# In layer 1, the reciprocals of the softmax sums and their store each move ahead of one step of x's quantisation

## The reference

```python
# layer 1, attention: 16 heads of 64, keys and values from ctx and one null key
attn = softmax(q * scale @ k.T)          # sums over 129 keys
out  = layernorm((attn @ v) @ Wo)
x = x + out
# layer 1, feed-forward: 128 -> 512 -> 128, rows quantised to 127 steps by their own largest value
def act_quant(x):
    s = 127 / clip(max(|x|, axis=-1), 1e-5)
    return clip(round(x * s), -128, 127) / s
x = x + bitlinear(silu(bitlinear(xn, w_gate)) * bitlinear(xn, w_up), w_down)
```

## Time and profile before

| what | value |
|---|---|
| median of 3 runs | 813.28 us (813.21 to 814.16) |
| the profiled execution, its own time | 821.97 us |
| its span | 820.2 us, mean granted TensorE clock 0.975 |
| TensorE (PE) busy | 775.9 us, 95% |
| VectorE (DVE) busy | 661.5 us, 81% |
| GpSimd (POOL) busy | 479.6 us, 58% |
| ScalarE (ACT) busy | 436.1 us, 53% |
| a_rT, the 32 reciprocals | 950 ns each, first at 338.5 us, last at 793.8 us |

### The profile page before, as it was taken

One profiled execution on the slowest core, in us unless ns is written; L12 is line 12 of the kernel. 1 busy time (PEld: TensorE's weight loads), 2 busy tenths in 40 slices (PEclk: granted clock), 3 DMA queues, 4 the chain that ended last, 5 costly groups with the idle time before them and its releaser, 6 DMA issues.

```text
span 820.2 us, 28896 instructions
## 1 busy us (share of the span) xinstructions
PE 775.9 (95%) x10878; PEld 655.3 (80%) x10908; DVE 661.5 (81%) x1747; ACT 436.1 (53%) x1049; POOL 479.6 (58%) x912
## 2 busy tenths in 40 slices
PE   8999999998898997999999999999999999999983
PEld 6777777776698996888888888888888888888861
DVE  6888989877756664578889888888898888988876
ACT  4666666656065773445455554554554545545542
POOL 7767678887856773335554654654655646555234
PEclk9999999989999999999999999999999999999995
DMA  8986220000421211112132231231221222213110
GB/s 245 374 331 255 102 86 15 16 21 28 142 72 49 64 50 36 38 50 64 48 77 57 54 81 47 54 82 46 67 69 48 81 52 55 81 48 76 42 39 14
DMA packets 72892, 66.76 MB, mean 81 GB/s; under 512 B 28354, under 2 KB 53682, under 8 KB 72754
## 3 DMA queue, kind: packets, MB, share of 16 engines
q1 hardware_dynamic: 57890, 40.66, 18.0%
q10 hardware_dynamic: 12816, 20.06, 6.6%
q0 software_dynamic: 2048, 4.20, 1.7%
HBM read 35.89 MB, written 24.37 MB: 73 GB/s over the span
## 4 chain that ended last, share of the span: by engine, by line
PE 49%; DVE 22%; SPq 11%; DMA 10%; issue 5%; ACT 1%; POOL 1%; DVEq 1%; another core or an unknown queue 0%; POOLq 0%; ACTq 0%
DMA a_r_all<-a_r_rows 7%; SPq L1483 4%; PE psum L1039 4%; PE psum L432 4%; PE psum L421 3%; DVE a_mxf L2231 3%; PE psum L1027 3%; PE psum L414 3%; PE psum L1807 3%; SPq L1462 3%; PE psum L1915 3%; PE psum L1881 2%; SPq L1467 2%; PE psum L1834 2%; DVE f_h L2317 2%
## 5 line engine op out<-in xcount | busy, mean ns | idle before, releaser
L2090 ACT ACTIVATE a_pT<-psum 128x512 f32<-128x512 f32 x128 | 69.5, 594 | 63.4 <-PE psum L1902 41.1
L1589 POOL TENSOR_TENSOR f_hd<-f_hmc,a_wmean 128x1 f32<-128x1 f32 x32 | 6.8, 212 | 135.5 <-DVE f_hr L2328 134.3
L720 DVE TENSOR_REDUCE l_mx<-psum 128x4 bf16<-128x512 f32 x128 | 81.8, 681 | 4.5 <-PE psum L403 2.9
L2231 DVE TENSOR_REDUCE a_mxf<-psum 128x8 f32<-128x1024 f32 x64 | 77.5, 1210 | 5.3 <-PE psum L1871 5.3
L1807 PEld LDWEIGHTS psum<-a_xT,a_Wq 128*128 128x128 f32 x512 | 66.5, 197 | 18.2 <-issue 14.1
L1819 PEld LDWEIGHTS psum<-a_cTm,a_Wk 128*128 128x128 f32 x512 | 64.3, 192 | 13.9 <-issue 13.9
L552 ACT ACTIVATE l_pT<-psum 128x512 f32<-128x512 f32 x128 | 70.6, 597 | 8.5 <-PE psum L421 8.2
L1807 PE MATMUL psum<-a_xT,a_Wq 128*128 128x128 f32 x512 | 73.2, 288 | 0.6 <-ACT a_xT L2073 0.6
L1583 POOL TENSOR_SCALAR f_hq<-f_ht 128x512 bf16<-128x512 f32 x31 | 60.4, 1947 | 19.9 <-ACT f_ht L2133 19.8
L1881 PE MATMUL psum<-a_qT,a_kT 64*128 64x128 f32 x1024 | 71.5, 280 | 0.0
L1849 PE MATMUL psum<-a_Wv,a_cTm 128*128 128x512 f32 x128 | 69.7, 630 | 0.0
(11 more groups left out here) (315 smaller groups left out, 2075.4 us busy)
## 6 DMA issues: line engine op xcount, KB each, us to landing
sorted_x<-r_zeros ACTq DMA_DIRECT2D x12, 1408.0 KB, 6.9
a_r_all<-a_r_rows SPq DMA_DIRECT2D x124, 128.0 KB
e_xt<-sorted_x SPq DMA_DIRECT2D x39, 64.0 KB, 1.8
sorted_y<-e_yt ACTq DMA_DIRECT2D x39, 64.0 KB, 1.6
e_w<-in_E_W1b SPq DMA_DIRECT2D x1, 2064.0 KB
a_cin<-in_ctx SPq DMA_DIRECT2D x32, 64.0 KB, 2.5
out<-f_x SPq DMA_DIRECT2D x32, 64.0 KB, 2.2
x_res<-in_x SPq DMA_DIRECT2D x1, 512.0 KB, 5.6
```

The lines of the kernel that those rows point to most:

```text
L720: nc.vector.tensor_reduce(mx[:, s, Q4 * k:Q4 * k + Q4], maxp[k % 2].rearrange("p (h t) -> p h t", h=Q4), AX_X, ALU.max).then_inc(mx_ready, 1)
L2090: nc.scalar.activation(pT[:, 2 * half + e, :], tp[e], ACT.Exp, scale=SCALE).then_inc(exp_ready, 1)
L2231: nc.vector.tensor_reduce(mxf[:, 8 * half:8 * half + 8].rearrange("p (e h) -> p e h", e=2), psum[:, 0:2, :].rearrange("p e (h t) -> p e h ...
```

## The change

Two calls change places, one on VectorE and one on SyncE. On VectorE `inverse(b)` is called ahead of `quantise_x(b - 2)`. On SyncE `store_reciprocals(b)` is called ahead of `turn_x(b - 2)`. No instruction is added or removed, and no function is changed.

```diff
@@ sync_part, in the loop over b
             if 1 <= b and b + 3 < B:
                 context(b + 3)
+            if b + 1 < B:
+                store_reciprocals(b)
             if 2 <= b < LAST + 2:
                 turn_x(b - 2)
-            if b + 1 < B:
-                store_reciprocals(b)
             if 3 <= b < H_LAST + 3:
                 turn_h(b - 3)
@@ vector_part, in the loop over b
             if f is not None:
                 multiply(f)
                 h_range(f)
+            inverse(b)
             if b >= 2:
                 quantise_x(b - 2)
-            inverse(b)
             if b < 3:
                 weight_signs(b)
```

## The result

The changed kernel takes 818.45 us (median of 17 runs, 814.43 to 821.88); the kernel before, run beside it, 814.16 us (17 runs, 811.55 to 817.78). The ratio is 1.0045, 95% interval 1.0027 to 1.0063: it is slower, by some 3.7 us between the means (2.2 to 5.1; the medians lie 4.3 apart). The forecast was 816.0, slower, with a range of 811.6 to 820.5.

What follows compares the result with a forecast made beforehand. TensorE was taken to set the 14.70 us even period, with late spreads making other periods late. First block +0.7, last block +1.0 and loop +1.0 gave +2.7 on 813.28: 816.0 us, range 811.6 to 820.5.

Steps and rivals of the forecast that it cites:

- VectorE's half, even period: Even period of layer 1's loop: reciprocal idles 0.78 us for its sums, L2258 keeps 0.14 us of cover, no cost.
- The lock: Rival, chance 0.03: f_xn blocks until GpSimd's rounding ends, 0.8 us in each of 27 blocks, +22 us, giving 837.
- the prediction's +0.35: In quantise_x's new place, f_xn or f_xt pays 0.35 us under GpSimd's rounding, or both do.
- SyncE's half: SyncE's queue in layer 1's loop: store moves ahead of xq's wait, spread issued 1.04 us later, less room for late landings.
- The ends: First affected block, b = 2, costs +0.7 us; last block, b = 31, costs +1.0 us.
- The loop: Layer 1's loop: 4.4 us for late landings less 3.4 us given back, net +1.0, between -3.4 and +8.
- Given back are the losses of today, 3.4 us: Layer 1's loop: today's late-period losses fall away with the wait for a_rT and the slow stores.
- The other term, 4.4 us: Layer 1's loop: landings late beyond 0.8 us cost TensorE the excess, including a few that were hidden before.
- I am wrong if late periods become rarer: The prediction's closing sign against itself, to be read in layer 1's loop in the changed kernel's profile.
- The loop pays in every block: Rival, chance 0.14: SyncE's and VectorE's ring binds, +0.34 us a block, +8.8 in some 26 blocks; 823.8 with the ends.
- The cure: Rival, chance 0.15: TensorE stops waiting for a_rT and slow stores vanish, -3.4 us in the loop; 811.6 with the ends.
- the sides cancel: Rival, chance 0.18: the loop gives back what the ends cost, -1.7 + 1.7 us, leaving 813.3.

Runs made afterwards that it cites:

- the two repeats of before: The kernel before, unchanged, executed twice more: 382.94 and 382.92 us for the 26 periods from pass 3 to 29, against 386.39 in its first trace.
- each half of the change alone: Only the VectorE call moved, or only the SyncE call moved, each against the kernel before: ratios 1.0162 and 1.0275.
- the loop of 383.3 without the spread: Changed order with the four spread DMAs issued for block 0 alone: ratio 1.0007 to the kernel before; old order with the same cut: 0.9964.

## Why the prediction was right, and where it was not

**VectorE's half, even period.** Right. The reciprocals wait for L1928 in 21 periods (0.54 in the even one, 0.78 forecast), L2258 keeps 0.21 of cover (0.14 forecast), the period stays 14.72. The lock for the whole of the rounding did not come: in the even period f_xn took 0.25 under it and f_xt 0.55, and over all 32 f_xn the longest was 0.687. The ratio and the even period both exclude +22 us. A shorter hold does exist (last section), and the prediction's +0.35 was one instance of it.

**SyncE's half.** Right in kind: spread 0.87 later behind the sums (1.04 forecast), `normalise` waiting 22, 30 and 26 times in three traces against 12, 12 and 6.

**The ends.** Right: +0.81 and +0.9, against +0.7 and +1.0.

**The loop.** The net, +1.0, is near what was found (1.3 us between the means of the four traces of each order, 385.1 and 383.8; 2.2 against an undisturbed loop of 382.9), but both of its terms were mis-sized. The step that failed is "Given back are the losses of today, 3.4 us": it took one execution's late periods for the kernel's habit, and in three of four executions there is nothing to give back. The other term, 4.4 us for the late landings of the new order, measured 1.2 to 3.7. Both were too large and they have opposite signs, so that the net came out near: that is luck. Likewise "I am wrong if late periods become rarer" could not be judged against that trace: seven of the 26 periods are over 14.8 in it, and six in the changed kernel's, while the two repeats of before have none.

With 1.7 for the ends, 1.3 to 2.2 for the loop make 3.0 to 3.9 us, and 3.7 was measured. The forecast of 2.7 lay one microsecond low, through the loop if through anything: it is inside the interval of 2.2 to 5.1.

**The rivals.** *The loop pays in every block* is not what happens: the new order's ring is 13.63 us, not longer than the old by 0.34 but shorter by 0.19, since behind a late landing the quantisation runs faster in its new place than where it stood: in the late periods above f_xt takes 0.29 for 0.65, and f_xn 0.25 for 0.33. But the mechanism is real, and each half of the change alone shows it. *The cure* had it right that max_scores stops waiting and that slow stores are hidden. What it had wrong is their worth: both repeats of before have no wait of the weight loads of max_scores, and the first has 8 waits for the store, 6.1 us together, in a loop that loses nothing. What *the sides cancel* needed, a loop that gives 1.7 back, no trace shows.

So the change is slower because it pays twice, neither time in the even period: 1.7 us at the ends, where quantise_x had been done under a wait for the sums and now stands behind it, and 1 to 2 us in the loop, where the later spread has little room left for a slow landing. That the loop's part goes through the landing rests on the waits of `normalise` and on the loop of 383.3 without the spread, one trace each; the two timed ratios are too wide to show it.

## What to carry to other kernels

For work that is passed round between engines and a queue, work out two numbers: how late a transfer may be before the bounding engine notices, and how much shorter than a period the ring is, which is how fast lateness is made up. A move can be free in the even period and cost 2.7% when it takes the second number to zero, as SyncE's half did, and the two halves of a change may each be dear and together cheap. Before a gain is booked from the late periods of one trace, look whether a second trace has them.

Where a long instruction waits for a result, cut the independent work around it so that as much as needed to cover the wait stands ahead, and the rest behind: here three instructions ahead and three behind cost no idle time on either side. First and last passes, where the cover is of another size, deserve the order that fits them.

## What the runs showed of the hardware

The landing of the same four DMAs of 128 KB differs by more than 2 us from block to block, and its late ones from execution to execution of one program: with identical instructions the 26 periods took 386.4, 382.9 and 382.9 us. In one late period a 16 KB instruction packet lay beside it; that it was the cause was not tested.

What GpSimd's rounding of the hidden rows does to f_xt and f_xn depends on where in it they start. The prediction put f_xt's 0.64 down to the rounding beside it, and overlap alone is not enough: in the late period of the changed kernel f_xt lies wholly inside the rounding and takes its shortest time, while in another period f_xn starts with the rounding and takes 0.69 instead of 0.25:

```profile
477.88 1.95 POOL L1583 TENSOR_SCALAR f_hq<-f_ht 128x512 bf16<-128x512 f32 x1 [0.67 <-ACT f_ht L2133]
...
477.88 0.69 DVE L2292 TENSOR_SCALAR f_xn<-x_res,a_ag,f_rs 128x128 f32<-128x128 f32 x1
...
567.20 1.95 POOL L1583 TENSOR_SCALAR f_hq<-f_ht 128x512 bf16<-128x512 f32 x1 [0.67 <-ACT f_ht L2133]
...
568.04 0.29 DVE L2301 TENSOR_SCALAR f_xt<-f_xn,f_rc 128x128 f32<-128x128 f32 x1
```

Taken over all fourteen traces of this case, the ends are pinned. All 215 f_xn and f_xt that started 0.02 to 0.40 us behind the start of the rounding ended 0.69 to 0.70 behind it, whenever they had started; all 103 f_xt that started 1.3 to 1.74 behind it ended 2.02 to 2.03 behind it, the 0.55 of the even period above among them (582.37 + 0.55 = 580.90 + 2.02); and all 118 f_xt that started 0.75 to 0.97 behind it took 0.29. So such an instruction is held until a fixed point if it starts in one of two stretches of the rounding, and not held between them. In the order of before f_xt started some 0.05 behind the rounding in 28 of the 32 blocks, which is the worst place; in the late period of the changed kernel it started 0.84 behind it. That is most of what made the new ring shorter. Whether the rounding itself holds it, or something that runs in step with the rounding, no run here tests.
